# Scaled parts of the vector messages: from two engines to ScalarE and TensorE alone

## The reference, cut to what matters

```python
w = ssp(edge_attr @ W_f1) @ W_f2 * (ssp(s0 @ W_s1) @ W_s2)
w1, w2, w3, w4 = jnp.split(w, 4, axis=-1)
x0e, x1e = split_irreps(x[edge_src])
sh0, sh1 = (edge_sh[:, 0], edge_sh[:, 1:4])
out0 = w1 * x0e * sh0[:, None] + w4 * (jnp.einsum('eum,em->eu', x1e, sh1) / jnp.sqrt(3.0))
out1 = w2[:, :, None] * x0e[:, :, None] * sh1[:, None, :] + w3[:, :, None] * x1e * sh0[:, None, None]
out = jax.ops.segment_sum(merge_irreps(out0, out1), edge_dst, num_segments=old_x.shape[0])
```

## Time and profile before

| | |
|---|---|
| median of 3 runs | 1619.62 us (1617.2 to 1623.02) |
| the profiled execution | 1620.53 us |
| its span in the trace | 1618.2 us |
| edge loop of the interaction layer | from 876.07 us (first near matmul) to 1463.7 us (last `take_sums`) |

### The profile page before, as it was taken

One profiled execution on the slowest core, in us unless ns is written; L12 is line 12 of the kernel. 1 busy time (PEld: TensorE's weight loads), 2 busy tenths in 40 slices (PEclk: granted clock), 3 DMA queues, 4 the chain that ended last, 5 costly groups with the idle time before them and its releaser, 6 DMA issues. The chain is left out here.

```text
span 1618.2 us, 21654 instructions
## 1 busy us (share of the span) xinstructions
PE 1416.6 (88%) x6471; PEld 830.5 (51%) x6471; DVE 1203.9 (74%) x2024; ACT 767.3 (47%) x1989; POOL 705.5 (44%) x744
## 2 busy tenths in 40 slices
PE   5599899899997769999565899999999999985998
PEld 3255577444445468999543344444444444443443
DVE  8976588523043979898454999999999999997023
ACT  2155355200001178889421676776776776761100
POOL 0000499267710664000003777777777777750000
PEclk9899999999997878889777999999999999997999
DMA  8993000000001035000114444444444444410101
GB/s 229 47 130 123 1 2 1 1 12 16 16 4 46 0 118 77 8 1 1 33 44 164 132 149 136 136 144 138 135 149 135 136 147 135 137 40 1 59 14 39
DMA packets 96960, 122.70 MB, mean 76 GB/s; under 512 B 49915, under 2 KB 78225, under 8 KB 96849
## 3 DMA queue, kind: packets, MB, share of 16 engines
q1 hardware_dynamic: 80497, 49.79, 16.8%
q0 software_dynamic: 16352, 71.55, 14.4%
HBM read 100.94 MB, written 11.59 MB: 70 GB/s over the span
## 5 line engine op out<-in xcount | busy, mean ns | idle before, releaser
L1412 POOL DMA_INDIRECT far<-far_rows,far_node x150 | 166.8, 1112 | 106.7 <-DVE far_node L1571 72.7
L432 POOL TENSOR_SCALAR hot_i<-iota_row,il 128x128 f32<-128x128 bf16 x125 | 108.2, 884 | 180.3 <-DVE il L454 172.1
L613 POOL DMA_INDIRECT records<-recs,place_i x136 | 136.6, 1004 | 87.5 <-issue 40.8
L1541 ACT ACTIVATE pair<-f_ps,recs 128x256 f32<-128x256 f32 x150 | 72.2, 481 | 164.5 <-PE s_ps L1488 164.5
L1041 PE MATMUL sum_ps<-wx,prob_t 128*128 128x65 f32 x1024 | 137.9, 294 | 12.5 <-DVE prob_t L1073 12.5
L1041 PEld LDWEIGHTS sum_ps<-wx,prob_t 128*128 128x128 f32 x1024 | 135.7, 213 | 14.2 <-DVE prob_t L1073 14.1
L1552 ACT ACTIVATE far<-far,recs 128x128 f32<-128x128 f32 x450 | 140.9, 408 | 0.0
L1454 PE MATMUL near_ps<-table,hot_t 128*128 x300 | 120.8, 526 | 9.4 <-DVE hot_t L1581 9.3
L708 PE MATMUL gcn_ps<-pair,hs 128*128 128x512 f32 x256 | 113.1, 604 | 3.2 <-DVE hs L771 3.2
L367 PE MATMUL perm_ps<-hot_high,hot_low 128*128 128x400 f32 x272 | 96.6, 518 | 20.2 <-ACT hot_high L237 20.2
L1488 PE MATMUL f_ps<-w,soft 32*128 32x512 f32 x300 | 84.5, 640 | 29.8 <-DVE soft L1603 29.8
(11 more groups left out here) (324 smaller groups left out, 3297.6 us busy)
## 6 DMA issues: line engine op xcount, KB each, us to landing
places<-local_rows SPq DMA_DIRECT2D x75, 128.0 KB, 4.3
pair<-zeros SPq DMA_DIRECT2D x1, 8576.0 KB, 59.6
s_all<-s_rows SPq DMA_DIRECT2D x8, 512.0 KB, 7.8
records<-empty_record SPq DMA_DIRECT2D x1, 2925.0 KB, 72.6
far<-far_rows,far_node POOLq DMA_INDIRECT x150, 4.9
recs<-in_edge_attr SPq DMA_DIRECT2D x1, 2176.0 KB, 26.9
records<-recs,place_i POOLq DMA_INDIRECT x136, 2.2
w_gcn<-in_L_gnn_W_gcn SPq DMA_DIRECT2D x2, 1024.0 KB, 7.8
```

The costliest lines, as they stand in the source:

```text
L432: nc.gpsimd.tensor_scalar(hot_i[:, g % 2, k, 1, :], c.iota_row[:], il[:, t + k:t + k + 1], None, ALU.is_equal).then_inc(hot_i_ready, 1)
L613: c.nc.gpsimd.indirect_dma_start(c.rows[:, :], bass.IndirectOffsetOnAxis(ap=c.place_i[:, t:t + 1], axis=0), c.recs[:, t, :], None).then_in ...
L1412: nc.gpsimd.indirect_dma_start(far[:, u % UNROLL, k, :], None, c.far[:, :], bass.IndirectOffsetOnAxis(ap=far_node[:, t:t + 1], axis=0)) \
```

## The change

All six (k, m) are given to ACT, and DVE has none. For that the message buffer has nine slots for each tile instead of eight, RAW moves to slot 8, and both matmuls of L1501 are now 512 columns wide (slots 4 to 7). To make room, `inner` goes from two buffers to one, so `add_inner` waits for the `turn` of the super-tile before.

```diff
-    BY_ACT = ((0, 1), (0,))
-    BY_DVE = tuple(tuple(m for m in range(3) if m not in taken) for taken in BY_ACT)
-    SLOTS = 8
-    ADDED, RAW = 4, 7
+    BY_ACT = ((0, 1, 2), (0, 1, 2))
+    SLOTS = 9
+    ADDED, RAW = 4, 8
...
-        inner = sb("inner", [P, 2, TPS, MUL])
+        inner = sb("inner", [P, TPS, MUL])
...
-        msg = (c.pair[:, (NB + 4) * FB:(NB + 8) * FB, 0, :].rearrange("p (k a) v -> p k a v", k=TPS),
+        msg = (c.pair[:, (NB + 4) * FB:(NB + 4) * FB + TPS * SLOTS, 0, :].rearrange("p (k a) v -> p k a v", k=TPS),
                sb("messages", [P, TPS, SLOTS, MUL])[:])
...
-                b, r = u % 2, u % UNROLL
+                r = u % UNROLL
                 pool.wait_ge(prod_ready, u + 1)
-                freed(pool, turned, u, 2)
-                nc.gpsimd.tensor_tensor(inner[:, b, :, :], far[:, r, :, 0:MUL], far[:, r, :, MUL:2 * MUL], ALU.add) \
+                freed(pool, turned, u, 1)
+                nc.gpsimd.tensor_tensor(inner[:], far[:, r, :, 0:MUL], far[:, r, :, MUL:2 * MUL], ALU.add) \
                     .then_inc(ip_ready, 1)
...
-                    nc.tensor.transpose(inner_ps[:, k * P:k * P + P], inner[:, u % 2, k, :], c.ident[:])
+                    nc.tensor.transpose(inner_ps[:, k * P:k * P + P], inner[:, k, :], c.ident[:])
...
-                dve.wait_ge(thirds_ready, u + 1)
-                dve.wait_ge(firsts_ready, u + 1)
-                for k in range(TPS):
-                    for m in BY_DVE[k]:
-                        at = R_SH + 1 + m
-                        nc.vector.scalar_tensor_tensor(
-                            of[:, k, 1 + m, :], of[:, k, RAW, :], c.recs[:, u * TPS + k, at:at + 1], of[:, k, 1 + m, :],
-                            ALU.mult, ALU.add)
                 dve.wait_ge(step, u * 2 + 2)
```

More of the change, by code:

```diff
@@ L1423, in add_inner @@
             def add_inner(u):
-                b, r = u % 2, u % UNROLL
+                r = u % UNROLL
                 pool.wait_ge(prod_ready, u + 1)
-                freed(pool, turned, u, 2)
-                nc.gpsimd.tensor_tensor(inner[:, b, :, :], far[:, r, :, 0:MUL], far[:, r, :, MUL:2 * MUL], ALU.add) \
+                freed(pool, turned, u, 1)
+                nc.gpsimd.tensor_tensor(inner[:], far[:, r, :, 0:MUL], far[:, r, :, MUL:2 * MUL], ALU.add) \
                     .then_inc(ip_ready, 1)
                 pool.wait_ge(ip_ready, u * 2 + 1)
-                nc.gpsimd.tensor_tensor(inner[:, b, :, :], inner[:, b, :, :], far[:, r, :, 2 * MUL:3 * MUL],
+                nc.gpsimd.tensor_tensor(inner[:], inner[:], far[:, r, :, 2 * MUL:3 * MUL],
                                         ALU.add).then_inc(ip_ready, 1)
```

## The result

The changed kernel takes 1637.07 us in the median of four runs (1633.62 to 1639.46), the kernel before 1618.41 us in the median of four. The ratio is 1.011, 95% interval 1.008 to 1.0139: slower by 1.1%. The two profiled spans differ by 16.4 us (1634.6 against 1618.2), where 17.7 were forecast; the edge loop itself is 17.4 us longer, and what lies ahead of it and behind it came out 0.2 and 0.8 us shorter.

A forecast was written before the change was run, and what follows sets the result against it. DVE, 99.5% busy, bounds the kernel at 7.574 us an iteration; PE then takes over at 7.81 us. 69 x 0.24 = 16.6 us plus 1.1 us at the ends gives 17.7 us, so 1637.3 us, range 1631 to 1647.

The forecast's parts named there:

- PE's slack: Steady loop: PE alone needs 7.17 us of the 7.57 us iteration, so it lies 0.40 us behind DVE.
- the price of the columns: L1501 on PE: 384 more columns, in two passes each, add 0.64 us an iteration, bounded at 0.55 and 0.74 us.
- The iteration of 7.81 us: Steady loop after the change: PE's 7.17 + 0.64 us sets the pace, 0.24 us more in each of 69 iterations.
- The ends: Loop's first and last iterations, outside the 69 steady ones: together +1.1 us.
- the stretch forecast at -0.67: Loop's end, before the last two `add_up`: one stretch still goes by DVE and gets 0.67 us shorter.
- DVE after the change: Steady loop: DVE waits over 1 us for `sum_ps` and `near_ps`, L1628 nears 0.7 us, busy share 86% or less.
- when DVE comes a microsecond later, most of it is gone: L1628 on DVE: its 1.73 us contain a hold by POOL's `thirds`, which mostly goes when DVE runs later.
- DVE's 6.90 us: Steady loop: without three fused passes, 0.67 us less, DVE could run at 6.90 us an iteration instead of 7.57.
- PE has room: Rival on PE's stream: added columns are hidden, kernel gets faster, 1592 or 1573 us; chance 0.04.
- A wait inside the 6.22 us: Rival, no change within 5 us: PE's 6.22 us contain a wait for ACT's `attr_t` before L1474, 1623 us; chance 0.05.
- the 6.96 us from 1441.10 to 1448.06: Iteration at the loop's end, taken as PE's own time with no wait at its end: +0.64 us.
- ACT or POOL late: Rival, slower by more: late `take_turned` or `product` makes PE wait at L1474 or L1464, 1648 us with 0.15 us; chance 0.07.

The follow-up runs named there:

- e7: Kernel before with POOL's `thirds` cut to 8 of 128 numbers a slot from the third super-tile on: ratio 0.9821, iteration 7.18 us.
- e4: Kernel before in the changed memory layout (nine slots, RAW in slot 8, one buffer of `inner`), same work on each engine: ratio 0.999, iteration 7.57 us.
- e8: Changed kernel with POOL's `thirds` cut to 8 of 128 numbers a slot from the third super-tile on: ratio 1.0099 against the kernel before, iteration 7.82 us.
- e2: Changed kernel with PE's two matmuls left at 384 and 256 columns: 1588.80 us, ratio 0.9792 against the kernel before.
- e1: Kernel before with both L1501 matmuls 512 columns wide and nothing else changed: 1645.76 against 1621.84 us, ratio 1.0152.
- e6: Kernel before in the changed layout, ACT making all six scaled parts, DVE's passes and PE's columns kept: ratio 0.9994, iteration 7.57 us.

## Why the prediction was right

**PE's slack and the price of the columns** carried the number. The slack of 0.40 us was read from starts, not from busy shares, and the runs without a hold (e7, 7.18 us) confirm the 7.17. The price of 0.64 us came out as 0.64. The iteration of 7.81 us was measured as 7.82: from the `filters` of iteration 8 (918.94 us) to that of iteration 77 (1458.53), 69 iterations take 539.6 us against 522.6 before, +17.0 where +16.6 were forecast.

That the median, 1637.07 us, lies 0.2 us from the forecast is luck. The kernel before came out at 1618.41 us in the median of four, 1.2 us under the one that the forecast was added to, so the medians differ by 18.7 us for 17.7, and the spans by 16.4.

**The ends** were forecast at +1.1 us and came to 17.4 - 17.0 = +0.4, as a sum of misses. What lies ahead of the steady part gave +0.6 instead of -0.2. Iterations 5 to 7 gave -0.5, and iteration 4, which the forecast put at no change, took 7.28 us for 6.07. In the changed kernel the granted clock was 0.76 in the mean of iteration 4 and 0.79 in iteration 5; before it was 1.00 in both and 0.80 in iteration 6. The drain's iteration 77 gave +0.63 (forecast +0.64). What follows gave -0.9 instead of +0.6. Rows of the changed kernel's timeline:

```profile
895.91 1.07 PE L1487 MATMUL f_ps<-w,soft 32*128 32x512 f32 x2
...
903.83 0.59 PE L1487 MATMUL f_ps<-w,soft 32*128 32x512 f32 x2
...
1472.44 1.10 PE L1497 MATMUL sum_ps<-messages,hot 128*128 128x512 f32 x2 [1.55 <-ACT messages L1562]
...
1475.09 1.02 PE L1502 MATMUL sum_ps<-messages,hot 128*128 128x512 f32 x2
...
1480.92 0.69 DVE L1644 TENSOR_TENSOR pair<-pair,sum_ps 128x512 f32 x1 [3.97 <-PE sum_ps L1502]
```

The same two passes take 1.07 us in iteration 5 and 0.59 us in iteration 6; and the last `add_up` but one ends with two passes in 1.02 us, where before they took 1.86 (row above; the granted clock of 1454 to 1460 us was 0.72 in the mean, and 1.00 here). So the last two `add_up` gave -0.4 for +1.28. Ahead of them PE waits 1.55 us for ACT's six passes (L1562), where before it waited for DVE: the stretch forecast at -0.67 gave -0.4. It is the one place in the loop where ACT's added passes are on the path, and their 0.88 us is the most that they can cost there, once. Ends of a microsecond or two are below what such a forecast can give.

**ACT** was right in the steady part: 1.6 us idle forecast, 1.58 measured, busy 419.34 / 530 = 79% for 80%. **`inner` and the layout** cost nothing (e4).

**DVE after the change** was wrong in a part that the sum did not need. Forecast were waits of over 1 us, at `near_ps` too, an L1628 nearer 0.7 us, and a busy share of 86% or less. Measured are 0.85 us, none at `near_ps`, 1.75 us and 88%. The failed step is "when DVE comes a microsecond later, most of it is gone". It left out that `thirds` waits for `add_up` as well, so that with PE late both `thirds` and `take_sums` start together at 1153.76 and the hold stays whole. Where the hold is taken out (e8), the rest of that forecast comes true: DVE waits 1.50 us at `add_up` and 0.34 us at `near_ps`, and is 76% busy. For the same reason DVE's 6.90 us was no pace that could be had. In e2 `thirds` starts 0.20 us after `filters` (1151.69 and 1151.89), `shift` ends 6.97 us after that, and the next `filters` comes at 1158.92, 7.23 us after the first: with PE's columns left out the iteration was 7.21 in the mean and not PE's 7.18.

**The rivals.** "PE has room" is refuted by e1 and by a PE without gaps in the changed kernel. The Trainium skill (Perfetto Trace Analysis, Identifying the Most-Contended Engine) names the share of weight loads as one of two measures of PE's distance from its limit. That share is 225.56 / 530 = 43% in a loop where PE demonstrably sets the time, and was 44% before, so here the measurement decides against it.

"A wait inside the 6.22 us" is settled by rows of the kernel before, one of the steady iteration and two of the drain:

```profile
1156.26 0.26 ACT L1518 COPY attr_t<-tail_ps 64x128 f32<-64x128 f32 x1
...
1443.83 0.26 ACT L1518 COPY attr_t<-tail_ps 64x128 f32<-64x128 f32 x1
...
1444.15 0.43 PE L1474 MATMUL tail_ps<-attr_t,w_f 64*64 64x128 f32 x2 [1.19 <-ACT attr_t L1518]
```

In the drain, where `gather_near` no longer stands ahead of it, L1474 starts 0.06 us after `attr_t` is written (1444.09). In the steady iteration `attr_t` is written at 1156.52 and L1474 starts at 1156.80, 0.28 us later. So ACT had been ready some 0.2 us before PE came to it, and the 0.54 us that PEld shows are not on the path. (These rows also show a slip of the prediction: the 6.96 us from 1441.10 to 1448.06 are not PE's own time, for they hold this wait of 1.19 us and no `gather_near`. The sum took only the +0.64 of `add_up` from there, which stands.)

"ACT or POOL late" is refuted by e6 for ACT, and for both by the changed kernel itself: in the steady part PE shows no wait at L1463 or L1473, and its 7.82 us are 7.18 + 0.64, with nothing left for a third party.

## What to carry to other kernels

When work moves from the busiest engine, measure the slack of the engine that receives it by the spacing of its starts, in an iteration where it waited for nobody. Here PE at 96% had 0.40 us, and 384 columns cost 0.64 us; giving it 128 columns (0.21 us) is a gain, 256 are even, 384 a loss. When two engines come within a few per cent of each other, look at what a buffer's release waits for: an early release of a part of the buffer took the mean iteration from 7.52 to 7.39 us (ratio 0.9957 to 0.9894), the moved pass from 7.57 to 7.52 us (1 to 0.9957). And an engine's 99.5% can contain time in which it is held, which no wait in the profile shows, but the same instruction's length elsewhere does.

## What the runs showed of the hardware

In these traces a POOL instruction on SBUF tiles holds two of DVE's instructions until about its end: L1628 takes 0.68 us alone and 1.72 to 1.76 us beside `thirds` in the steady loop, ending 0.55 us after it; the pair of L1589 takes 0.47 us alone, 0.97 us beside `add_inner` and 2.22 us beside `thirds`. L1653, which has one of its inputs in PSUM, takes 0.67 to 0.69 us throughout, beside `thirds` too. The Trainium skill (SBUF — State Buffer, SBUF: two separate sides) describes this as an exclusive lock between DVE and GpSimd on a shared pair of ports, held for a whole instruction; the traces agree for these forms.

A pass of a 32-bit matmul lasts 379, 486 and 592 ns for 256, 384 and 512 columns, and its start-to-start time falls and rises with the columns, at 0.84 ns each (1.08 us for 1280 columns of passes before, 1.72 us for 2048 in the changed kernel), though its weight load of 190 ns stays the same.
